# The last expert layer and its norm, joined in one block of work

## The reference

```python
top_val = jnp.max(gate_probs, -1); top_val = top_val / (top_val + 1e-08)
onehot = one_hot(argmax(gate_probs), 8)          # each token goes to one of 8 experts
ye = gelu(xe @ expert_w1) @ expert_w2
out = einsum('end,ne->nd', ye, onehot) * top_val[:, None]
mu = mean(out); var = mean((out - mu) ** 2)      # over the 128 numbers of a token
out = (out - mu) * rsqrt(var + 1e-05) * ln_gamma + ln_beta
x = x + out
```

## Time and profile before

| | us |
|---|---|
| median of 3 runs (3142.51 to 3147.43) | 3144.14 |
| the profiled execution | 3145.59 |
| its span in the profile | 3143.6 |
| busy in the span: PE, DVE, ACT, POOL | 2537.9, 2182.5, 1836.1, 1768.5 |

### The profile page before, as it was taken

One profiled execution on the slowest core, in us unless ns is written; L12 is line 12 of the kernel. 1 busy time (PEld: TensorE's weight loads), 2 busy tenths in 40 slices (PEclk: granted clock), 3 DMA queues, 4 the chain that ended last, 5 costly groups with the idle time before them and its releaser, 6 DMA issues. The chain is left out here.

```text
span 3143.6 us, 102802 instructions
## 1 busy us (share of the span) xinstructions
PE 2537.9 (81%) x30076; PEld 2002.7 (64%) x30077; DVE 2182.5 (69%) x7900; ACT 1836.1 (58%) x5856; POOL 1768.5 (56%) x1934
## 2 busy tenths in 40 slices
PE   4964689489999889988999983389759999979571
PEld 2843677367777678865777762377637777748561
DVE  5976622478888857727888887642179999979525
ACT  3841144279999723347999975124348888857220
POOL 2822277457777645025787762047637777748171
PEclk9975699789999989988999996579979999999585
DMA  2002355411111130002333320135534544500132
GB/s 102 3 1 77 114 153 155 120 39 40 39 40 40 28 128 0 0 1 64 79 79 80 78 52 0 65 95 152 136 95 116 116 115 115 116 7 3 51 106 69
DMA packets 195621, 225.55 MB, mean 72 GB/s; under 512 B 24708, under 2 KB 166020, under 8 KB 194405
## 3 DMA queue, kind: packets, MB, share of 16 engines
q1 hardware_dynamic: 182788, 197.56, 23.7%
q0 software_dynamic: 12672, 25.98, 3.1%
HBM read 201.68 MB, written 21.76 MB: 71 GB/s over the span
## 5 line engine op out<-in xcount | busy, mean ns | idle before, releaser
L1763 POOL TENSOR_TENSOR sx<-sx,rs 128x1028 f32<-128x1028 f32 x384 | 732.1, 1906 | 280.0 <-DVE rs L1911 280.0
L1856 ACT ACTIVATE sx<-sx,nm 128x257 f32<-128x257 f32 x1536 | 771.5, 506 | 115.6 <-DVE nm L1899 115.5
L1899 DVE CUSTOM_DVE_ANT_0 sx<-bank,rows 128x257 f32<-128x257 f32 x1024 | 411.0, 421 | 52.2 <-PE bank L1846 49.2
L1567 ACT ACTIVATE hT<-bank,B 128x128 f32<-128x128 f32 x714 | 206.0, 368 | 277.8 <-PE bank L1535 270.8
L350 POOL TENSOR_TENSOR rstd<-var,nhalf 128x8 f32<-128x8 f32 x48 | 79.0, 1645 | 423.9 <-DVE var L381 423.9
L1856 ACT ACTIVATION_READ_ACCUMULATOR sx<-sx,nm 128x1 f32 x1536 | 290.8, 189 | 0.0
L1846 PE MATMUL bank<-kT,qb 32*128 32x257 f32 x3072 | 279.3, 429 | 0.0
L1918 DVE COPY pt<-bank 128x512 f32<-128x512 f32 x384 | 263.8, 687 | 2.1 <-PE bank L1781 1.7
L1781 PE MATMUL bank<-C,sx 128*128 128x128 f32 x1536 | 251.7, 286 | 3.0 <-POOL sx L1763 3.0
L1800 PEld LDWEIGHTS bank<-W,ct 128*128 128x128 f32 x1536 | 219.0, 192 | 54.2 <-DVE nm L1899 20.3
L1794 PE MATMUL bank<-ct,W 128*128 128x257 f32 x768 | 235.7, 389 | 16.9 <-DVEq L1886 15.3
(11 more groups left out here) (381 smaller groups left out, 5728.6 us busy)
## 6 DMA issues: line engine op xcount, KB each, us to landing
ct<-in_ctxT SPq DMA_DIRECT2D x384, 128.5 KB
W<-in_L_w SPq DMA_DIRECT2D x159, 256.0 KB
rows<-rows_x SPq DMA_DIRECT2D x256, 128.5 KB
keep<-rows_keep SPq DMA_DIRECT2D x128, 128.5 KB
yg<-copy_outs SPq DMA_DIRECT2D x40, 256.0 KB
token_rows<-XN SPq DMA_DIRECT2D x24, 256.0 KB, 2.3
W<-in_L_w SPq DMA_DIRECT2D x1, 6144.0 KB, 16.9
W<-in_L_w SPq DMA_DIRECT2D x39, 128.0 KB
```

The costliest lines, as they stand in the source:

```text
L1763: pool.tensor_tensor(sx[:, j, :, 0:KEYS], sx[:, j, :, 0:KEYS], rs[:, j, :].unsqueeze(2).to_broadcast([P, 4, KEYS]), ALU.mult).then_inc(p_r ...
L1856: ins = act.activation(sx[:, j, h, 0:KEYS], sx[:, j, h, 0:KEYS], ACT.Exp, bias=nm[:, j, h:h + 1], scale=-1.0, accum_out=sm[:, j, h:h + 1])
L1899: dve.tensor_tensor_reduce(sx[:, j, h, 0:KEYS], B[h][:, 0:KEYS], add, -1.0, 3.0e38, ALU.add, ALU.min, nm[:, j, h:h + 1]).then_inc(s_summed ...
```

## The change

The block that brings the rows back is left out for this layer (`sparse_experts` returns ahead of it), and `norm_affine_add` runs inside `moe`, behind the experts. It now loads `copy_outs` by quarters straight into `Y`. The gate is no longer multiplied in: with g the gate, the variance of the gated row is g*g times that of the row, so `var` is multiplied by `g2`, and the scale `rstd` by g; `nmr` is minus the mean times that scale. GpSimd makes the scale with a power, as in `norm`; ScalarE applies it in place in `Y`; VectorE multiplies by gamma and adds to X. Beta is added to X earlier: in `place`, TensorE spreads gamma and beta, ScalarE copies them to `gb`, and GpSimd adds beta to X in eight operations of 128x512. The loops over groups are written out. The core of the diff (the functions of before stand above):

```diff
-def place(E, K, M, token_of, copy_of, expert_of, blocks, fetch):
+def place(E, K, M, token_of, copy_of, expert_of, blocks, fetch, gb=None):
...
+        rows_psum, rows_ready = sig("c_done", 1 if gb else 0), sig("d_done", 1 if gb else 0)
         @block.sync
         def _(sp):
             fetch(sp)
 
+        if gb:
+            @block.scalar
+            def _(act):
+                act.wait_ge(*rows_psum(1))
+                act.copy(gb[:].rearrange("p a n -> p (a n)"), B[5][:, 0:2 * P]).then_inc(rows_ready.sem, 1)
+            @block.gpsimd
+            def _(pool):
+                st_ = Steps(pool, sig, "pool_step")
+                pool.wait_ge(*rows_ready(1))
+                for gr in range(GROUPS):
+                    xg = X[:, gr * GT:(gr + 1) * GT, :]
+                    st_.count(pool.tensor_tensor(xg, xg, gb[:, 1, :].unsqueeze(1).to_broadcast([P, GT, P]), ALU.add))
+                st_.wait()
+                st_.close()
         @block.tensor
         def _(pe):
+            if gb:
+                pe.matmul(B[5][:, 0:P], ones_row, r("gamma"), start=True, stop=True)
+                pe.matmul(B[5][:, P:2 * P], ones_row, r("beta"), start=True, stop=True).then_inc(rows_psum.sem, 1)
...
+        if Y is not None:
+            return
         RING = 4
...
+        if Y is not None:
+            norm_affine_add(Y, g[0], gb)
...
-def norm_affine_add(Y):
+def norm_affine_add(Y, g, gb):
...
+        QT = TILES // 4
+        st, var, dif, nmr, g2 = sb2("stats", [P, TILES, 6]), *(sb2(n, [P, TILES]) for n in ("var", "dif", "nmr", "g2"))
+        nhalf = sb2("nhalf", [P, QT])
+        y_loaded = [sig(f"stored{q}", 1) for q in range(4)]
+        var_ready, rstd_ready, scale_ready, stat_ready = (sig(n, 4) for n in ("var_ready", "rstd_ready", "scan_ready", "stat_ready"))
+        xn_ready, x_added, stored = sig("xn_ready", GROUPS), sig("x_added", GROUPS), sig("stored", GROUPS)
+        outs = T["copy_outs"][0:TILES * P, :].rearrange("(t p) d -> p t d", p=P)
+        @block.sync
+        def _(sp):
+            for q in range(4):
+                sp.dma_start(Y[:, q * QT:(q + 1) * QT, :], outs[:, q * QT:(q + 1) * QT, :]).then_inc(y_loaded[q].sem, 16)
+            for gr in range(GROUPS):
+                sp.wait_ge(*x_added(gr + 1))
+                sp.dma_start(ot[:, gr * GT:(gr + 1) * GT, :], X[:, gr * GT:(gr + 1) * GT, :]).then_inc(stored.sem, 16)
+            sp.wait_ge(*stored(GROUPS))
+        @block.gpsimd
+        def _(pool):
+            for q in range(4):
+                qs = slice(q * QT, (q + 1) * QT)
+                pool.wait_ge(*var_ready(q + 1))
+                pool.tensor_tensor(rstd[:, qs], var[:, qs], nhalf[:], ALU.pow).then_inc(rstd_ready.sem, 1)
+                pool.wait_ge(*rstd_ready(q + 1))
+                pool.tensor_tensor(rstd[:, qs], rstd[:, qs], g[:, qs], ALU.mult).then_inc(scale_ready.sem, 1)
+                pool.wait_ge(*scale_ready(q + 1))
+                pool.tensor_tensor(nmr[:, qs], mean[:, qs], rstd[:, qs], ALU.mult).then_inc(stat_ready.sem, 1)
         @block.scalar
         def _(act):
+            for gr in range(GROUPS):
+                act.wait_ge(*stat_ready(gr // 2 + 1))
+                for t in range(gr * GT, (gr + 1) * GT):
+                    ins = act.activation(Y[:, t, :], Y[:, t, :], ACT.Identity, bias=nmr[:, t:t + 1], scale=rstd[:, t:t + 1])
+                ins.then_inc(xn_ready.sem, 1)
         @block.vector
         def _(dve):
             st_ = Steps(dve, sig, "dve_step")
+            st_.count(dve.memset(nhalf[:], -0.5))
+            st_.count(dve.tensor_tensor(g2[:], g[:], g[:], ALU.mult))
+            def finish(gr):
+                dve.wait_ge(*xn_ready(gr + 1))
+                yg = Y[:, gr * GT:(gr + 1) * GT, :]
+                xg = X[:, gr * GT:(gr + 1) * GT, :]
+                st_.link(dve.tensor_tensor(yg, yg, gb[:, 0, :].unsqueeze(1).to_broadcast([P, GT, P]), ALU.mult))
+                dve.tensor_tensor(xg, xg, yg, ALU.add).then_inc(x_added.sem, 1)
+            for q in range(4):
+                qs = slice(q * QT, (q + 1) * QT)
+                dve.wait_ge(*y_loaded[q](1))
+                for t in range(q * QT, (q + 1) * QT):
+                    st_.count(dve.bn_stats(st[:, t:t + 1, :], Y[:, t:t + 1, :]))
+                st_.wait()
+                st_.count(dve.tensor_tensor(dif[:, qs], st[:, qs, 1], st[:, qs, 4], ALU.subtract))
+                st_.count(dve.scalar_tensor_tensor(out=mean[:, qs], in0=st[:, qs, 1], scalar=-1.0, in1=st[:, qs, 4],
+                                                   op0=ALU.mult, op1=ALU.subtract))
+                st_.link(dve.tensor_tensor(var[:, qs], st[:, qs, 2], st[:, qs, 5], ALU.add))
+                st_.count(dve.tensor_scalar(mean[:, qs], mean[:, qs], 0.5, None, ALU.mult))
+                st_.link(dve.scalar_tensor_tensor(out=dif[:, qs], in0=dif[:, qs], scalar=0.25, in1=dif[:, qs],
+                                                  op0=ALU.mult, op1=ALU.mult))
+                st_.link(dve.scalar_tensor_tensor(out=var[:, qs], in0=var[:, qs], scalar=1.0 / P, in1=dif[:, qs],
+                                                  op0=ALU.mult, op1=ALU.add))
+                st_.link(dve.tensor_tensor(var[:, qs], var[:, qs], g2[:, qs], ALU.mult))
+                dve.tensor_scalar(var[:, qs], var[:, qs], EPS, None, ALU.add).then_inc(var_ready.sem, 1)
+                if q == 3:
+                    finish(0)
+                    finish(1)
+            for gr in range(2, GROUPS):
+                finish(gr)
```

More of the change, by code:

```diff
@@ L1620, in _ @@
                                 t = gr * GT + j
[L1621 to L1625, removed]
+                                ins = dve.scalar_tensor_tensor(out=X[:, t, :], in0=yg[:, gr % RING, k, j, :], scalar=g[k][:, t:t + 1],
+                                                               in1=X[:, t, :], op0=ALU.mult, op1=ALU.add)
                                 if k == K - 1 and j == GT - 1:
@@ L1643, in moe @@
                 b2s = sb2("b2s", [P, E, P]) if b2 is not None else None
+                gb = sb2("gb", [P, 2, P]) if Y is not None else None
                 loads = 2 + (b2 is not None)
@@ L1658, in moe @@
                     route(kind, E - (kind == "capacity"), gw, bias_row, (*M, *g))
-                    place(E, K, M, token_of, copy_of, expert_of, blocks, fetch)
+                    place(E, K, M, token_of, copy_of, expert_of, blocks, fetch, gb)
                     sparse_experts(E, K, FC, w1, kept, W2, B1, b2s, w2_loaded(loads), g, token_of, copy_of, expert_of, blocks, Y)
+                if Y is not None:
+                    norm_affine_add(Y, g[0], gb)
         def xattn(name):
@@ L1992, in sb2 @@
                     return hold(c2, n, shape)
[L1993 to L1997, removed]
-                block = c2.enter_context(nc.Block())
-                @block.tensor
@@ L2001, in _ @@
-                def _(pe):
-                    pe.matmul(B[0][:, 0:P], ones_row, r("gamma"), start=True, stop=True)
-                    pe.matmul(B[0][:, P:2 * P], ones_row, r("beta"), start=True, stop=True).then_inc(a_done.sem, 1)
+                QT = TILES // 4
+                st, var, dif, nmr, g2 = sb2("stats", [P, TILES, 6]), *(sb2(n, [P, TILES]) for n in ("var", "dif", "nmr", "g2"))
+                nhalf = sb2("nhalf", [P, QT])
+                y_loaded = [sig(f"stored{q}", 1) for q in range(4)]
@@ L2015, in _ @@
                     st_ = Steps(dve, sig, "dve_step")
[L2016 to L2042, removed]
@@ L2043, in _ @@
-                    st_.close()
[L2045 to L2050, removed]
+                    st_.count(dve.memset(nhalf[:], -0.5))
+                    st_.count(dve.tensor_tensor(g2[:], g[:], g[:], ALU.mult))
@@ L2076, in program @@
             moe("first", 8, 1, 2, TILES + 8 - 1, GW3[:], None, T["L3_w1"], T["L3_b1"], T["L3_w2"], None, False, Y)
-            norm_affine_add(Y)
 def layout(inputs):
```

## The result

The changed kernel took 3124.57 us (median of 4 runs, 3124.19 to 3125.09), the kernel before 3144.36 us beside it (3142.51 to 3147.43): a ratio of 0.9941, 95% interval 0.9928 to 0.9953. The forecast was 3125.0. In the profiles the span went from 3143.6 to 3122.7 us, 20.9 less.

| stretch | before | after | difference |
|---|---|---|---|
| start to SP's weight fetch in `place` (code unchanged) | 2953.51 | 2951.40 | -2.1 |
| weight fetch to the experts' first gather | 26.94 | 33.06 | +6.1 |
| first gather to the end of the last scatter's instruction | 100.61 | 100.41 | -0.2 |
| last scatter to the first load's issue | 8.28 | 8.28 | 0.0 |
| first load's issue to the end of the span | 54.26 | 29.55 | -24.7 |

The account below looks back on a forecast made before the run. The prediction took VectorE, behind the loads, to bound the kernel's end. It summed -25.6 us there and +6.5 in `place` to -19.1: 3126.5 from the profiled 3145.59, 3125.0 against the median 3144.14; range 3122 to 3128, chance 0.62.

Parts of the forecast that it names:

- The end: Last block, from the first load of expert rows to the end of the span: 25.6 us gained.
- Statistics: VectorE's chain in the last block: 2.80 us for each of four quarters, loads hidden behind it.
- finish: VectorE's gamma multiplication and X add at the end: eight groups of two operations, 10.8 us.
- the first landing: Arrival of the first quarter's expert rows: at 3093.1, after issue at 3089.34; bounds 3092.3 and 3099.7.
- The matmuls in `place`: Two matmuls ahead of TensorE's counting matmuls, on which VectorE waits: 0.9 us, between 0 and 1.26.
- The adds: GpSimd's eight adds in `place`: one VectorE operation passes per add; 6.5 us late, the matmuls' 0.9 among them.
- Rival 1: In `place`, GpSimd's adds cost nothing, only the matmuls do: 3119.4 us; chance 0.10.
- Rival 2: In the last block, the four loads share the engines and land together at 3099.7: 3131.6 us; chance 0.10.
- Rivals 4 and 5: In `place`: adds of 2.18 us, 3131.2, chance 0.05; adds above 3.6 us, slower than before, chance 0.03.
- ScalarE doesn't pace the end: Case judged: in the last block ScalarE paces instead of VectorE, at 0.6 a normalization: 3128.8 us, inside the range.
- Rival 3: In VectorE's finish, GpSimd's last power holds the shared port, 2.1 us more: 3127.1 us; chance 0.07.
- The total: Whole kernel: -25.6 at the end plus 6.5 in `place`, -19.1 us; 3125.0 against the median.

## Why the prediction was right

- *The end, 25.6 forecast, 24.7 measured.* Statistics 11.2 and 11.19; finish 10.8 and 10.71; the last add ends 2.75 us before the span does, 2.9 forecast. The mis-sized term is the first landing, 3.76 forecast, 4.90 measured and 4.04 to 5.42 in the other profiles. It was read from one profile of smaller loads, for a time that the other profiles show to vary.
- *The matmuls in `place`, 0.9 forecast, 1.05 measured*, with ScalarE's copy, in the run without adds.
- *The adds, 5.6 forecast, 5.06 measured.* One operation of VectorE passes per add, as the earlier trace rows had it for other shapes; the run with sixteen shows the same mechanism carrying on.
- *Rival 1* (adds free) is refuted by the run without them, 5.06 us. *Rival 2* (the four loads land together): no idle on VectorE after the first landing. *Rivals 4 and 5* needed adds of 2.18 and 3.6 us; the longest took 1.65. ScalarE doesn't pace the end: it is done 2.7 us early.
- *Rival 3* (the power holds the port): beside the power of 2.01 us VectorE's operations take 0.68 and 0.69 like all the others. GpSimd is what slows there: the power grew from 1.64 in the quarters before it, and the two small multiplications behind it from 0.20 to 0.54 and 0.53. The Trainium skill, page "SBUF — State Buffer", section "Who interferes with whom", says that a VectorE operation with two SBUF inputs contends with a GpSimd one that reads SBUF, and that one with a single input, outside its two-port modes, does not: the scan at 0.95 and the reduction at 0.42 beside the adds agree. The `tensor_scalar` at 0.69 and the casts of the run with sixteen adds have one input and lengthen; in which mode they ran no row shows. The Trainium skill also says there, of VectorE's two-port modes, that the first to issue holds the pair for the whole instruction. The prediction took this for every operation on the port. No run here shows VectorE held for the whole of a power, and operations of the plain two-input kind got through within it.
- *The total* came out at -19.8 in the medians where -19.1 was forecast, but the parts that the change touches moved by -18.6. The two misses, 0.9 us at the end and 0.4 in `place` as a whole, have opposite signs, and the rest is the spread of unchanged code: that the median lies only 0.4 us from the forecast is in part luck.

What the forecast didn't say is that one of its parts was worth nothing: its own terms, 6.5 us in `place` against 8 x 0.73 at the end, already showed that.

## What to carry to other kernels

Work handed to an idle engine can slow the engine that works beside it: here the same eight GpSimd adds cost 5.06 us beside VectorE's chain and nothing beside TensorE's matmuls, so price the neighbour, not only the idle engine. Set each moved term's gain against its own cost, as here 5.8 against 6.1, before adding up the change. When a wait is taken away, ask who else waits for the same event: the loads could go 6.9 us sooner, but VectorE waited for the same block to end, and another 3.2 us came only when that boundary went too.

## What the runs showed of the hardware that was not expected

- A block boundary behind the scatters is dear and steady: 8.27 to 8.29 us from the end of the last scatter's instruction to the first load's issue in the next block, in all ten profiles with the loads there. Where SP waits for the scatters' landing alone, it issues after 1.40 to 1.42 us; the rest went with the boundary.
- Beside a GpSimd add, casts of 128x32 go from 0.18 to 0.68 and 1.19 us, one of 1x39 from 0.17 to 1.12, and a `tensor_scalar` of 128x8 from 0.17 to 0.69, though they have one input; reductions (0.42) and the copies from PSUM (0.49) keep their time. The two-input operations of 128x512 beside the 128x8 power keep theirs (0.69), and the power lengthens (1.64 to 2.01).
- The landing of the same first load varies by 1.4 us between the eight profiles that have it (4.04 to 5.42), while the stretch from the first statistic to the last X add, where its code is unchanged, repeats to 0.04 us (21.89 to 21.93).
